# A transformer layer on one core: hand-written orders of five engines rearranged in the prologue, a square swapped with a staging copy, and the gate product one slot later

## What is computed

```python
b, s1, _ = x.shape                       # x: 4 x 512 x 512, y = ctx_1024: 4 x 512 x 256
y_dca = y[:, -DCA:, :]                   # DCA = 16 extra keys
y_main = y[:, :-DCA, :]
kv_dca = (y_dca @ Wkv_dca + bkv_dca).reshape(b, DCA, 2, H, HD)
k_dca = _ln(kv_dca[:, :, 0], kn_dca_w, kn_dca_b)
v_dca = kv_dca[:, :, 1]
q = _ln((x @ Wq + bq).reshape(b, s1, H, HD), qn_w, qn_b)      # H = 16 heads of HD = 32
kv = jnp.concatenate([y_main @ Wk + bk, y_main @ Wv + bv], axis=-1)
k = _ln(kv[..., :HD], kn_w, kn_b)
ctx = attn(q, k, v) + attn(q, k_dca, v_dca)
x = x + ctx @ Wo + bo                    # the attention was given layernorm(x)
...
gate = ghost(x, gate_idx, lut)           # weight = lut[idx], INTER = 1376
up = ghost(x, up_idx, lut)
h = silu(gate) * up
x = x + ghost(h, down_idx, lut)
```

## Time and profile before

| | us |
|---|---|
| median of 3 runs | 815.9 |
| the runs | 815.7, 817.7, 815.9 |
| the profiled execution | 815.7 |
| its span from first to last instruction | 813.8 |

### The profile page before, as it was taken

One profiled execution on the slowest core, in us unless ns is written; L12 is line 12 of the kernel. 1 busy time (PEld: TensorE's weight loads), 2 busy tenths in 40 slices (PEclk: granted clock), 3 DMA queues, 4 the chain that ended last, 5 costly groups with the idle time before them and its releaser, 6 DMA issues.

```text
span 813.8 us, 14816 instructions
## 1 busy us (share of the span) xinstructions
PE 760.2 (93%) x5842; PEld 312.0 (38%) x5842; DVE 516.4 (63%) x1003; ACT 493.6 (61%) x1000; POOL 241.2 (30%) x253
## 2 busy tenths in 40 slices
PE   2887785999999999999999999999999999999998
PEld 1342231333443343334543342235433433265445
DVE  7979999898868992316669962228499810153211
ACT  3488888888547985662668866635488856511100
POOL 6883111001752221004742220036512200014320
PEclk9998998999999999999999999999999999999999
DMA  7739896595420002212200003223000000100001
GB/s 254 195 105 290 222 274 179 127 184 138 130 55 1 1 2 52 66 39 75 57 2 1 1 14 77 54 66 53 2 1 1 1 27 27 40 14 1 0 14 39
DMA packets 73253, 58.60 MB, mean 72 GB/s; under 512 B 33313, under 2 KB 60705, under 8 KB 73057
## 3 DMA queue, kind: packets, MB, share of 16 engines
q1 hardware_dynamic: 72848, 57.40, 27.4%
q10 hardware_dynamic: 208, 0.26, 0.1%
q0 software_dynamic: 128, 0.00, 0.0%
HBM read 41.72 MB, written 9.50 MB: 63 GB/s over the span
## 4 chain that ended last, share of the span: by engine, by line
PE 74%; DVE 18%; ACT 4%; issue 3%; POOL 1%; DVEq 0%; POOLq 0%; ACTq 0%
PE ps L1551 49%; PE ps L1876 8%; PE ps L1857 6%; PE ps L1602 5%; DVE arena L1038 3%; DVE nmax L1348 3%; PE ps L1828 3%; DVE nmax L1347 3%; DVE nmax L1342 2%; ACT ps L924 2%; PE ps L1863 2%; PE ps L1748 2%; DVE arena L1045 1%; DVE arena L1053 1%; DVE arena L1346 1%
## 5 line engine op out<-in xcount | busy, mean ns | idle before, releaser
L1551 PE MATMUL ps<-arena,wf_hi 128*128 128x512 f16 (+2 forms) x736 | 211.1, 371 | 4.1 <-DVE arena L1053 3.4
L924 ACT ACTIVATE ps<-ps,nmax 128x496 f32<-128x496 f32 x256 | 166.0, 651 | 23.1 <-DVE nmax L1347 23.1
L956 ACT ACTIVATE arena<-ps 128x1024 f32<-128x1024 f32 x128 | 124.3, 1026 | 73.8 <-PE ps L1863 73.8
L1551 PE MATMUL ps<-arena,wf_lo 128*128 128x512 f16 (+2 forms) x368 | 136.1, 370 | 0.0
L1551 PE MATMUL ps<-wf_hi,arena 128*128 128x512 f16 (+3 forms) x374 | 114.9, 368 | 0.0
L655 POOL TENSOR_TENSOR hrstd<-hvar,mhalf 128x16 f32<-128x16 f32 (+1 forms) x33 | 100.0, 3043 | 44.8 <-DVE hvar L1142 44.6
L1551 PEld LDWEIGHTS ps<-arena,wf_hi 128*128 128x128 f16 (+1 forms) x736 | 69.4, 100 | 90.3 <-DVE arena L1053 14.3
L1038 DVE TENSOR_SCALAR arena<-arena,wf_lo 128x2048 f16<-128x2048 f16 (+1 forms) x132 | 90.8, 749 | 3.8 <-PE ps L1602 3.6
L613 POOL TENSOR_TENSOR xrstd<-xvar,mhalf 128x1 f32<-128x1 f32 x32 | 23.7, 742 | 209.3 <-DVE xvar L1080 209.3
L1602 PE MATMUL ps<-arena,wf_lo 128*32 128x512 f16 (+1 forms) x1056 | 67.6, 401 | 9.4 <-ACT arena L778 3.6
L1551 PE MATMUL ps<-wf_lo,arena 128*128 128x512 f16 (+3 forms) x187 | 68.5, 366 | 0.0
(11 more groups left out here) (151 smaller groups left out, 1034.2 us busy)
## 6 DMA issues: line engine op xcount, KB each, us to landing
arena<-idx SPq DMA_DIRECT2D x124, 128.0 KB, 3.7
arena<-in_x SPq DMA_DIRECT2D x32, 256.0 KB, 3.0
wf_lo<-in_idx SPq DMA_DIRECT2D x10, 512.0 KB, 5.3
idx<-wf_hi SPq DMA_DIRECT2D x10, 384.0 KB, 3.5
out<-arena SPq DMA_DIRECT2D x15, 256.0 KB, 2.0
wf_lo<-in_idx SPq DMA_DIRECT2D x11, 256.0 KB, 6.7
arena<-in_ctxT SPq DMA_DIRECT2D x4, 512.0 KB, 5.5
arena<-in_Wq SPq DMA_DIRECT2D x4, 256.0 KB, 5.2
```

The source lines that it names most:

```text
L924: last = act.activation(sc, sc, ACT.Exp, bias=nmax[:, 0, t, h:h + 1], accum_out=den[:, 0, t, h:h + 1])
L956: act.activation(probs[n_ % 2][:, 2 * p:2 * p + 2, :], ps[:, bank:bank + 2, :], ACT.Exp).then_inc(s["probs_set"], 1)
L1551: last = pe.matmul(dst, l, r, start=(first and i == 0), stop=(stop and i == len(todo) - 1))
```

## The change

Six things change, all of them in order and none in what is computed:

- In the prologue of batch 0 the hand-written orders of VectorE, ScalarE and TensorE are rearranged: among others `values_low` comes before `key_centre`, `variance(0)` before `key_centre`, `extra_context_low` and `value_bias` later, and on TensorE the first two value products before the key projections 2 and 3, the extra keys' value product near the end.
- The two copies of the extra keys of batch 0 move from VectorE to GpSimd (`dca_keys(a)`), behind the last `rstd`.
- `convert(0)` on GpSimd waits for `wk_lo`.
- `normalise(8)` and `rescale(8)` move from inside stage one of batch 0 to before its first maxima and exps.
- At the start of batch 1 ScalarE squares unit 5 before it stages tile 2.
- `USE_AT` has lag 3 instead of 2: `use_gate` comes one slot later where gates lie in stage one, in batches 1 to 3.

```diff
-USE_AT = {it: later(slot_of(("gate", it, 1)), 2) for it in range(IT)}
+USE_AT = {it: later(slot_of(("gate", it, 1)), 3) for it in range(IT)}
...
@@ GpSimd, convert
-                if it > 1:
+                if it == 0:
+                    pool.wait_ge(s["wk_lo"], 1)
+                elif it > 1:
...
@@ GpSimd, dca_keys
-                pool.wait_ge(s["ST_done"], nth(bt, NR, 0))
+                if sum(bt):
+                    pool.wait_ge(s["ST_done"], nth(bt, NR, 0))
+                else:
+                    pool.wait_ge(s["tr_lo"], UNITS_0.index(("d", 0)) + 1)
...
@@ GpSimd, batch 0
                     for u in range(1, len(units)):
                         rstd(u)
+                    dca_keys(a)
                     convert(1)
...
@@ ScalarE, batch 1
                     stage(2, 1, prev)
+                    square(a, 5, False)
                     stage(2, 2, prev)
-                    square(a, 5, False)
                     stage(2, 3, prev)
...
@@ ScalarE, batch 0 (parts)
-                    context_hi(a, ctx_first, cT)
                     act.wait_ge(s["sq_eps"], 1)
                     square(a, 0, True)
+                    context_hi(a, ctx_first, cT)
...
                     rescale(7)
+                    rescale(8)
...
-                    if prev is None and m == 0:
-                        rescale(8)
...
@@ VectorE, batch 0 (parts)
                     key_sums()
-                    moments(1, 3, a, x_first[3])
+                    variance(a, 0)
+                    values_low()
                     key_centre()
-                    turn(1, 1, a, LB0[1])
-                    variance(a, 0)
                     context_lo(a, ctx_first, cT)
-                    value_bias()
                     key_low()
...
-                    dve.wait_ge(s["tr_lo"], UNITS_0.index(("d", 0)) + 1)
-                    for i in range(2):
-                        dve.tensor_copy(kT[i][:, :, 0:DCA], kd[i][:, :, 0:DCA]).then_inc(s["kd_set"], 1)
-                    normalise(a, 7, True)
...
                     low_half(6)
+                    normalise(a, 8, True)
...
-                        if m == 0:
-                            normalise(a, 8, True)
...
@@ TensorE, batch 0
+                    project_values(0)
+                    project_values(1)
                     project(2)
                     project(3)
-                    project_values(0)
+                    turn_heads(0)
+                    project_values(2)
                     turn(1, 2, a, LB0[2], x_first[2])
-                    project_values(1)
-                    turn_heads(0)
                     project(4)
                     turn_heads(1)
-                    project_values(2)
+                    project_values(3)
                     project(5)
                     turn_heads(2)
-                    project_values(3)
+                    project(6)
+                    turn_heads(3)
                     pe.wait_ge(s["lo1"], 3)
                     turn(1, 3, a, LB0[3], x_first[3])
-                    turn_heads(3)
-                    project(6)
+                    project(7)
                     turn_heads(4)
-                    project(7)
+                    project(8)
                     turn_heads(5)
-                    project(8)
+                    project_values(4)
                     turn_heads(6)
-                    project_values(4)
                     turn_heads(7)
```

More of the change, by code:

```diff
@@ L868, in core @@
                     query_hi(0)
+                    query_hi(1)
                     turn(1, 0, LB0[0])
-                    query_hi(1)
+                    turn(1, 1, LB0[1])
+                    query_hi(2)
                     act.wait_ge(s["b_cent"], 1)
@@ L899, in core @@
                     rescale(2)
+                    square(a, 6, True)
                     values(2)
+                    values(3)
+                    turn(1, 3, LB0[3])
                     rescale(3)
-                    square(a, 6, True)
-                    turn(1, 3, LB0[3])
+                    square(a, 7, True)
                     rescale(4)
-                    square(a, 7, True)
+                    square(a, 8, True)
                     rescale(5)
-                    values(3)
-                    square(a, 8, True)
                     rescale(6)
@@ L1271, in core @@
                     query_sums(0)
+                    standardise(1, 0, a, x_first[0], x_first[0])
                     query_centre(0)
                     query_sums(1)
-                    standardise(1, 0, a, x_first[0], x_first[0])
                     moments(1, 1, a, x_first[1])
-                    query_centre(1)
                     query_sums(2)
                     query_low(0)
-                    moments(1, 2, a, x_first[2])
+                    query_centre(1)
+                    query_sums(3)
                     query_centre(2)
-                    query_sums(3)
                     bias_sums()
                     standardise(1, 1, a, x_first[1], x_first[1])
+                    query_centre(3)
                     bias_centre()
-                    query_centre(3)
+                    turn(1, 0, a, LB0[0])
                     query_low(1)
-                    turn(1, 0, a, LB0[0])
                     query_low(2)
+                    query_low(3)
                     bias_low()
-                    query_low(3)
+                    moments(1, 2, a, x_first[2])
+                    turn(1, 1, a, LB0[1])
+                    moments(1, 3, a, x_first[3])
                     key_sums()
-                    moments(1, 3, a, x_first[3])
+                    variance(a, 0)
+                    values_low()
                     key_centre()
-                    turn(1, 1, a, LB0[1])
-                    variance(a, 0)
                     context_lo(a, ctx_first, cT)
-                    value_bias()
                     key_low()
                     standardise(1, 2, a, x_first[2], x_first[2])
-                    extra_context_low()
+                    normalise(a, 0, True)
                     variance(a, 1)
-                    normalise(a, 0, True)
-                    values_low()
-                    variance(a, 2)
                     extra_sums()
                     extra_centre()
+                    variance(a, 2)
                     parameters()
```

29 lines of the change are left out of this document (15 added, 14 removed).

## The result

| | us | ratio to the kernel before |
|---|---|---|
| before, the runs beside it | 816.0 (815.7 to 817.7) | |
| after | 821.66 (821.08 to 822.13) | 1.0061 [1.0046, 1.0076] |
| after again, two later sets | 820.95 and 820.79 | 1.0050 [1.0037, 1.0063] and 1.0048 [1.0035, 1.0062] |

By the ratios the change makes the kernel slower by 4 to 5 us (the plain differences of the medians, 5.7, 4.2 and 3.6 us, scatter more). Gains and losses in us are taken from the ratios from here on, where one is given. The forecast was +2.8 us (818.5, range 816.2 to 820.4): the sign was right, the size outside the range. The span of the profiled execution is 820.5 us, before 813.8. These 6.7 us are more than the medians say, since the profiled execution of before (815.7) was one of its quicker ones and that of the changed kernel (822.64) was its slowest.

A forecast was written before the change was run, and what follows sets the result against it. It took TensorE as the bound in the last two thirds, VectorE in batch 0's stage one, GpSimd's powers as the prologue's tightest chain. Prologue 0.5, swap 0.85 and use_gate 1.45 gave +2.8 on 815.7: 818.5 us, range 816.2 to 820.4.

The forecast's parts named there:

- the term for `wd_hi` and what hangs on it: Prologue: wd_hi, behind two value products and two key projections on TensorE, ends at 35.6, extra_low at 37.9 us.
- The powers: Prologue, GpSimd: each power is held until VectorE's two-operand operation ends, then takes 2.89 us; chain 0.8 us shorter.
- the rival of fixed durations: Prologue: powers keep their unit's old duration, VectorE's stream starts 1.8 us later; 819.8 us in all, chance 0.16.
- The copies and the scores: End of prologue: extra keys' copies behind rstd(8) hold scores(0) to 55.9, 1.2 us later; VectorE's stream starts 0.5 later.
- The cast's wait: Prologue, GpSimd: the cast waits for wk_lo and starts at 28.5, as before (28.59); rstd(1) would wait anyway.
- Part 2: Start of batch 1: squaring unit 5 before staging delays the transposes and first FFN piece, +0.85 us.
- Part 3: Stage one of batches 1 to 3: use_gate one slot later makes TensorE wait at gate pieces, +1.45 us.
- three such waits of 0.25 and one of 0.6: Stage one of batch 1, kernel before: TensorE's waits for use_up, said to make up 1.1 us.
- absorbed waits: Stage one: gate-piece waits come out of the up waits one for one, part 3 is 0; 817.1 us, chance 0.19.
- a wait at every gate piece: Stage one: all gate pieces wait with nothing absorbed, part 3 costs 5.0 us; 822.1 us, chance 0.04.

The follow-up runs named there:

- e17: The changed kernel once more, unaltered, timed in turn with its version with filler matmuls: 820.79 us, ratio 1.0048.
- e1: The changed kernel with 14 unused matmuls on TensorE ahead of the first value product of batch 0: 819.89 us, ratio 1.0034.
- e7: The changed kernel with 14 unused matmuls in the prologue and the extra keys' two copies back on VectorE, behind low_half(5): 819.28 us, ratio 1.0030.
- e8: The kernel before with 16 unused matmuls on TensorE behind the last exp of batch 0: 816.53 us, ratio 0.9997.
- e3: The kernel before with use_gate one slot later and nothing else: ratio 1.0017.
- e9: The kernel before with GpSimd's casts of the index blocks from the third on released one lookup later: 816.61 us, ratio 1.0000.

## Why the prediction was wrong in size

- **The step that failed** is the term for `wd_hi` and what hangs on it: "behind TensorE's two value products (1.3 us each, now ahead) and two key projections (1.5 each): 27.3 (`cT_lo`) + 5.8 = 33.1". I took the durations at full clock without asking what TensorE had done before them. The wait ahead of them stands in no term of the prediction. The first product started at 27.92, the value products took 5.28 and the projections ended at 36.5: 8.6 us for the predicted 5.8, and 7.5 in e17. At full clock, in e1, they took 5.8 (27.99 to 33.76), so the total was right for that clock, though the durations named add up to 5.6. With this `extra_low` ended at 41.24 (predicted 37.9), `rstd(3)` at 44.00 (40.7), the scores started at 59.00 (55.9) and the one-hots at 62.13 (59). `extra_low` was put 3.3 us too early for this execution and 2.2 for the four with a clock of 0.75. With the clock held it is 0.6, all from the start of the value products (27.99 for 27.3): `extra_low` ended at 38.52 in e1.
- **The warning was there**, in the trace of before: lookups of 3.59 and 3.31 us for 1.91, ahead of and behind the idle time at 135 us, and a mean clock of 0.90 over stage one of batch 0. The prediction took nothing from it for the prologue.
- **The powers** were right. "Held until VectorE's operation ends, then 2.89": `rstd(0)` 3.83 beside `values_low`, `rstd(1)` 2.90 where it was 3.88 before, so the rival of fixed durations is out. After a hold the rest measures 2.76 rather than 2.89 (41.24 to 44.00); it was to be seen before, where 24.80 + 0.93 is 25.73 and `context_lo` ended at 25.86.
- **The copies and the scores** were right: the copies are the last thing before the scores, at a price of 0.5 us (e7). The cast's wait cost nothing: GpSimd is idle again before `rstd(2)` (2.78 us in the changed kernel; 33.72 to 33.87 in e1). With the clock held the first one-hot still came 0.8 to 0.95 us later than before (its end and its start), not 0.5: the steps were some 0.4 us later than worked.
- **Part 2**: +0.85, measured 0.82 and 0.81 in traces, idle time 1.57 for 1.6. **Part 3**: +1.45, measured 1.62, with the waits on `use_gate` where they were put, at 0.24 us each. The prediction's "three such waits of 0.25 and one of 0.6" would be 1.35, not the 1.1 of the earlier trace rows: of each 0.25 the trace shows 0.18 as idle. The rivals of absorbed waits and of a wait at every gate piece are out. Timed alone, both agree within their intervals (+0.6, which is not clear of nothing, and +1.4).
- **The sum.** With the clock held the change costs +2.8 and +2.5 us (1.0034, 1.0031), for +2.8 predicted. That it meets the forecast so closely is in part luck: by the traces it is 0.83 + 0.82 + 1.62 = 3.3 us. The forecast lacked one rival, a clock that falls, at +1.4 us by the medians and 1.6 to 2.7 by the first one-hots of the traces. Why the medians show less than the traces, and none of it for the prologue alone, stays open.

## What to carry to other kernels

Before TensorE work is put behind a longer wait, look at what its engine does in that wait: three microseconds of idle time in the prologue made the next 3 to 7 us run at half clock, and the reordered products cost up to nearly twice their price (5.28 us for 2.75). A gap on an engine that is not the bound is free only if what comes behind it is not on the path. Look for ready work to put into the gap. Unused matmuls kept the clock up in all five profiles that had them in the prologue, and won 1.4 us in the whole change; with the prologue alone, and at the end of stage one, they won nothing that the times show.

## What was new about the hardware

- The length of the slow stretch differs between executions of one program: 0.51 or 0.75 over the same 6.9 us, behind idle time of 3.28 us (e17, the result), which moves the first one-hot by 1.1 us. One profile (e8) shows 0.50 from 24.2 us on, behind 2.11 us of idle time.
- A VectorE comparison of 128x2048 fp16 (0.74 us) takes up to 1.95 us beside a GpSimd cast of 128x1536 (e3), and 1.64 beside a GpSimd subtraction (e9). Maxima that read PSUM are not touched (1.18 us either way). That this makes executions differ by 2 us is not shown: without such meetings of casts, e9 was no faster.
- A GpSimd power of 128x16 does not slow down in proportion beside a two-operand VectorE operation; it ends 2.76 us after that operation does, whether it had started 0.16 us after it (4.89 us in all, e8) or 0.73 us (4.32, before). A power that runs already when such an operation starts keeps its 2.94 us (36.42 in the changed kernel, beside `extra_low` from 38.95).
